# Sliding-window attention: the values of two groups of heads in one go, and the output projection some steps later

## Chip, core and metric

The kernel runs on one core of a Trainium2 chip. The metric is the device time of one launch in microseconds (us), the median of three runs. The change touches one phase of a kernel of two transformer layers.

## What is computed

Two layers; each computes x + s * silu(ffn(xn)) with s an attention and xn the layer norm of x. The change is in the first layer's attention, on B = 2 sequences of S = 2048 tokens, D = 512, 16 heads of 32:

```python
k = (xn @ Wkv @ Wk); v = (xn @ Wkv @ Wv); q = xn @ Wq        # split into 16 heads
mask = (ki <= qi) & ((qi - ki < 128) | (ki < 16))            # a window, and 16 persistent keys
scores = einsum('bqhd,bkhd->bhqk', q, k) * 32 ** -0.5
attn = softmax(where(mask, scores, min))
s = einsum('bhqk,bkhd->bqhd', attn, v).reshape(B, S, D) @ Wo
```

The rest (experts of the first layer, a similarity attention and a shared and routed feed-forward of the second) runs in other phases, before and after.

## The kernel before

`phase_attend` works on 32 tiles of 128 queries. A tile has 16 heads, and each head is one *step*; the program of every engine is one unrolled list over the steps `s`, and `tile_of(s, offset)` gives the tile `u` whose step number `offset` (counted from its first head) is `s`. Work at offsets of 16 and more therefore falls between the heads of the following tile. Each engine executes its list in order, and engines wait for each other by semaphores.

What a head takes, by name:

- `score(s)` (TensorE, line 873): q times the keys of two blocks and the persistent ones, over 96 rows (three parts of 32), 288 columns. It is issued three steps ahead, and there are three PSUM banks for it (`SR = 3`), so it waits until L1033 of the score three before is done.
- `top(s)` (VectorE, L1033): scale, mask and row extremum, in one custom instruction. It needs a buffer that `exps` of three heads before must have read.
- `exps(s)` (ScalarE, L978): the exponential with its row sum; issued two steps ahead of `turn`.
- `turn(s)` (TensorE, L890): at each odd head four 128x128 transposes for two heads.
- `copy_out` (L1044 on VectorE, L988 on ScalarE for pairs 1, 3 and 5): the transposed probabilities to SBUF.

And per tile: `values(u, g)` (L903) multiplies the probabilities of four heads with their values; each of its eight multiplies has 32 columns of weights and writes its own 32 partitions of `psO`, in two passes, so sixteen are issued. `turn_sums` (L913) transposes the persistent keys' probabilities and the inverse row sums, `sums_out` (ScalarE, L994) copies them to `xT`, `spread` (L931) multiplies the inverse sums with a 0/1 matrix `sel` so that each head's inverse stands in its 32 partitions (`psR`, in the bank `psXY`), `inverse_out` (L1000) copies that, `pers_values` (L919) adds the persistent keys' part, `divide` (VectorE, L1057) forms `o`, `out_hi` (ScalarE, L1006) and `out_lo` (VectorE, L1061) split it in two parts, `project(u, c)` (L105 to L107, in the helper `mm3`) multiplies with Wo for c = 0 to 3 into `psXY`, and `finish` (L1068) copies the result. GpSimd gathers the persistent probabilities (L805), scatters token numbers for the later phase (L810) and stores the result (L827).

In steps of the running tile, modulo 16, the order is now: the third `values` of the tile before at 0, `turn_sums` at 1, `spread` at 3, the last `values` and `pers_values` at 4, `divide` at 5, `out_hi` and `out_lo` at 6, the first `values` of this tile at 8, the four parts of `project` at 9 to 12, the second `values` at 12 ahead of the last part, `finish` at 13. Within a step TensorE's order is score, turn, then these.

Waits that matter: `values(u, 0)` waits for `o_ready` of the tile before, since both use `psO`; `spread` waits for `x_out`; `project(u, 0)` waits for `o_split`.

Of the kernel before, what the change touches and what calls it, by code (L numbers as in the profile page):

```python
# [20 lines left out]
P = 128  # L21
# [11 lines left out]
NH, HD = 16, 32  # L33
# [574 lines left out]
def phase_attend(nc, env):  # L608
# [6 lines left out]
    ctx, sb, ps, sem = scope(nc)  # L615
# [4 lines left out]
    GH = 4  # L620
    NGR = NH // GH
# [10 lines left out]
    with ctx:  # L632
# [3 lines left out]
        kp = sb("a_kp", [ST, B, NH, PERSIST], F32R)  # L636
        vd = sb("a_vd", [P, B, 2, HD])
        vp = [sb(f"a_vp{i}", [P, 2, HH, HD]) for i in range(B)]
        sel = sb("a_sel", [NH, NGR, GH, HD])
        mask = [sb(f"a_mask{i}", [P, W]) for i in range(4)]  # L640
        rl = [sb(f"a_rl{i}", [P, P]) for i in range(2)]
        wo = [sb(f"a_wo{h}", [P, KC, D], F32R) for h in range(2)]
# [110 lines left out]
        xT = [sb(f"a_xT{i}", [P, 3 * P]) for i in range(2)]  # L753
# [16 lines left out]
        X_AT = 17  # L770
# [22 lines left out]
        def tile_of(s, offset):  # L793

            u, rest = divmod(s - offset, NH)
            return u if rest == 0 and 0 <= u < TILES else None
# [61 lines left out]
        def _(pe):  # L858
# [66 lines left out]
            def spread(u):  # L925
                pe.wait_ge(x_out, u + 1)
                if u:

                    pe.wait_ge(y_ready, u)
                for g in range(NGR):  # L930
                    ins = pe.matmul(psR[:, g, :], sel[:, g, :, :].rearrange("p j d -> p (j d)"),  # L931
                                    xT[u % 2][0:NH, 2 * P:3 * P], start=True, stop=True)
                ins.then_inc(spread_full, 1)

            def project(u, c):
# [11 lines left out]
            for s in STEPS:  # L947
                if s + SR < N:
                    score(s + SR)
                if s < N:  # L950
                    turn(s)
                for g in range(NGR):
                    if (u := tile_of(s, GH * g + GH - 1 + LAG)) is not None:
                        values(u, g)
                if (u := tile_of(s, X_AT)) is not None:
                    turn_sums(u)
                if (u := tile_of(s, X_AT + 2)) is not None:
                    spread(u)
                if (u := tile_of(s, X_AT + 3)) is not None:
                    pers_values(u)  # L960
                for c in range(KC):
                    if (u := tile_of(s, X_AT + 8 + c)) is not None:
                        project(u, c)

        @block.scalar
        def _(act):
# [23 lines left out]
            def sums_out(u):  # L990
                act.wait_ge(x_full, u + 1)
                if u >= 2:
                    act.wait_ge(pers_done, u - 1)
                act.activation(xT[u % 2][:, :], bank(u, HH)[:, 0:3 * P], ACT.Copy).then_inc(x_out, 1)  # L994
# [15 lines left out]
            for s in STEPS:  # L1010
                if s + SR - 1 < N:
                    exps(s + SR - 1)
                if s < N:
                    copy_out(s)
                if (u := tile_of(s, X_AT)) is not None:
                    sums_out(u)
                if (u := tile_of(s, X_AT + 3)) is not None:
                    inverse_out(u)
                if (u := tile_of(s, X_AT + 5)) is not None:
                    out_hi(u)  # L1020

        @block.vector
        def _(dve):
# [50 lines left out]
            for s in STEPS:  # L1074
                if s + SR < N:
                    top(s + SR)
                if (u := tile_of(s, X_AT - 3)) is not None:
                    invert(u)
                if s < N:
                    copy_out(s)  # L1080
                if (u := tile_of(s, X_AT + 4)) is not None:
                    divide(u)
                if (u := tile_of(s, X_AT + 5)) is not None:
                    out_lo(u)
                if (u := tile_of(s, X_AT + 12)) is not None:
                    finish(u)


# [1581 lines left out]
```

## Time and profile before

| | |
|---|---|
| median of three runs | 4498.79 us (4495.98 to 4507.62) |
| the profiled execution | 4549.09 us, span 4547.1 us |
| TensorE, weight loads | busy 4214.5 us, 3571.8 us |
| VectorE, ScalarE, GpSimd | busy 2097.8, 1663.2, 1354.6 us |
| granted TensorE clock, mean | 0.955 |
| the loop of `phase_attend` | about 398 to 958 us of the span |

Busy times of TensorE include a modelled end of each multiply, so neighbours overlap and the sum is above the time in which it issues. A number in square brackets behind an instruction in a timeline is the idle time of its engine before it, and after the arrow what ended it. Consecutive instructions of one kind are merged, with their count.

### The profile page before, as it was taken

What the parts mean: (1) busy time and instruction counts of PE and PEld (TensorE: products, weight loads), DVE (VectorE), ACT (ScalarE), POOL (GpSimd) and SP (SyncE); (2) the same over time, 40 slices, a digit from 0 to 9 for tenths busy, and PEclk for the clock granted to TensorE, in tenths of its full rate; (3) what the DMA queues carried; (4) which work ended last, traced back from release to release, by engine and by line L of the source; (5) the groups of instructions that cost most, each with busy time, mean ns of one, the idle gap of its engine ahead of it and who ended that gap; (6) DMA issues with size and microseconds to landing.
All of it is one profiled execution on the core that took longest, in us unless ns stands there. A gap on an engine that the chain in (4) does not pass through costs nothing. (4 is left out here: it accounts for less than half of the span.)

```text
span 4547.1 us, 69223 instructions
## 1 busy us (share of the span) xinstructions
PE 4214.5 (93%) x23045; PEld 3571.8 (79%) x23046; DVE 2097.8 (46%) x4010; ACT 1663.2 (37%) x3234; POOL 1354.6 (30%) x2020
## 2 busy tenths in 40 slices
PE   6975888879999999999997999998799999999998
PEld 5864666669989999998985777776578888788887
DVE  4457666644444444444444544453343333343333
ACT  2214666644334444444432333331232222222222
POOL 0012444445555555555551233333100000000000
PEclk8877999989999999999998999998899999999999
DMA  5767676636555556555554533431423222321221
GB/s 188 282 237 173 118 141 122 126 88 131 114 122 124 128 121 135 123 125 128 120 118 140 181 123 130 140 134 58 146 75 104 98 87 71 102 95 63 98 82 48
DMA packets 351911, 561.40 MB, mean 123 GB/s; under 512 B 33089, under 2 KB 198625, under 8 KB 347490
## 3 DMA queue, kind: packets, MB, share of 16 engines
q1 hardware_dynamic: 282770, 394.19, 29.3%
q0 software_dynamic: 68944, 164.62, 16.8%
q8 instruction: 120, 1.97, 0.2%
q14 instruction: 77, 0.63, 0.1%
HBM read 384.36 MB, written 174.34 MB: 123 GB/s over the span
## 5 line engine op out<-in xcount | busy, mean ns | idle before, releaser
L1227 POOL DMA_INDIRECT acc_d<-e_yw,e_to x208 | 336.0, 1615 | 284.9 <-ACT e_yw L1384 268.4
L2289 POOL DMA_DIRECT2D out<-d_res x32 | 17.4, 543 | 1304.8 <-DVE d_res L2521 1304.8
L2468 DVE TENSOR_TENSOR d_h<-d_sg,d_psU 128x512 f32<-128x512 f32 x144 | 98.9, 687 | 520.3 <-PE d_psU L107 461.9
L978 ACT ACTIVATE a_pr<-a_sm,a_nmax 128x272 f32<-128x272 f32 x512 | 264.0, 516 | 167.1 <-DVE a_nmax L1033 137.6
L105 PE MATMUL e_psG<-e_gu,e_xT 128*128 128x352 f32 x832 | 289.6, 348 | 11.4 <-DVE e_xT L1438 9.3
L1446 DVE TENSOR_TENSOR e_h<-e_sg,e_psU 128x352 f32<-128x352 f32 x208 | 108.3, 521 | 394.3 <-ACT e_sg L1397 379.9
L1033 DVE CUSTOM_DVE_ANT_0 a_sm<-a_psS,a_mask 128x272 f32<-128x272 f32 x512 | 212.7, 432 | 156.6 <-PE a_psS L873 140.2
L107 PE MATMUL e_psG<-e_gu,e_xT 128*128 128x352 f32 x832 | 271.9, 327 | 0.0
L106 PE MATMUL e_psG<-e_gu,e_xT 128*128 128x352 f32 x832 | 271.4, 326 | 0.0
L105 PE MATMUL e_psU<-e_gu,e_xT 128*128 128x352 f32 x832 | 271.0, 326 | 0.0
L106 PE MATMUL e_psU<-e_gu,e_xT 128*128 128x352 f32 x832 | 269.6, 324 | 0.0
L105 PE MATMUL e_psY<-e_wd,e_hT 128*128 128x512 f32 (+1 forms) x624 | 265.7, 426 | 1.2 <-DVE e_hT L1429 1.2
L107 PE MATMUL e_psU<-e_gu,e_xT 128*128 128x352 f32 x832 | 266.3, 320 | 0.0
L1197 POOL DMA_INDIRECT e_xs<-xn_d,e_idx x209 | 210.2, 1006 | 174.3 <-POOL e_idx L1194 168.3
L2396 ACT ACTIVATE d_hT<-d_h 128x512 fp32r<-128x512 f32 x144 | 91.0, 632 | 458.9 <-DVE d_h L2468 400.9
L107 PE MATMUL e_psY<-e_wd,e_hT 128*128 128x512 f32 (+1 forms) x624 | 247.1, 396 | 0.0
L1397 ACT ACTIVATE e_sg<-e_psG 128x352 f32<-128x352 f32 x208 | 96.4, 463 | 409.3 <-PE e_psU L107 406.5
L106 PE MATMUL e_psY<-e_wd,e_hT 128*128 128x512 f32 (+1 forms) x624 | 245.4, 393 | 0.0
L2390 ACT ACTIVATE d_sg<-d_psG 128x512 f32<-128x512 f32 x144 | 86.0, 598 | 423.0 <-PE d_psG L107 423.0
L1378 ACT ACTIVATE e_hT<-e_psH 128x384 fp32r<-128x384 f32 x208 | 102.1, 491 | 371.3 <-PE e_psY L107 199.5
L105 PE MATMUL d_psG<-d_x,d_gu 128*128 128x512 f32 x576 | 225.2, 391 | 12.6 <-DMA d_x<-xT_d 12.5
L105 PE MATMUL d_psU<-d_x,d_gu 128*128 128x512 f32 x576 | 227.5, 395 | 0.0
(429 smaller groups left out, 12067.1 us busy)
## 6 DMA issues: line engine op xcount, KB each, us to landing
d_gu_raw<-in_wgu SPq DMA_DIRECT2D x144, 512.0 KB, 3.2
qk_d<-f_qk SPq DMA_DIRECT2D x32, 1024.0 KB
a_q<-qk_d SPq DMA_DIRECT2D x96, 256.0 KB
a_k<-qk_d SPq DMA_DIRECT2D x96, 256.0 KB
e_rawgu<-in_w_gate SPq DMA_DIRECT2D x32, 704.0 KB
e_rawgu<-in_w_up SPq DMA_DIRECT2D x32, 704.0 KB
b_gu_raw<-in_wgu SPq DMA_DIRECT2D x40, 512.0 KB, 3.9
xT_d<-f_xT SPq DMA_DIRECT2D x16, 1024.0 KB
```

Of the source, the lines that this page charges most:

```text
L105: pe.matmul(out, lhs[0], rhs[1], start=first, stop=False, **kw)
L106: pe.matmul(out, lhs[1], rhs[0], start=False, stop=False, **kw)
L107: return pe.matmul(out, lhs[0], rhs[0], start=False, stop=last, **kw)
L978: act.activation(pr[half][:, h % HH, :], sm[s % SR][:, :], ACT.Exp, bias=nmax[s % SR][:, :], scale=-1.0, accum_out=rs[u % 2][:, h:h + 1]). ...
L1033: dve.tensor_tensor_reduce(out=sm[s % SR][:, :], in0=psS[s % SR][:, PERSIST:2 * KW], in1=m[:, :], scale=-SCALE, scalar=3.0e38, op0=ALU.add ...
L1197: pool.indirect_dma_start(rows[:, :], None, env.xn_d, bass.IndirectOffsetOnAxis(ap=idx[k][:, :].bitcast(U32), axis=0))\
L1227: pool.indirect_dma_start(env.acc_d, bass.IndirectOffsetOnAxis(ap=to[:, :].bitcast(U32), axis=0), yw[:, :], None, compute_op=ALU.add).then ...
L1378: act.activation(hT[0][:, :, :], psH[:, :, :], ACT.Copy).then_inc(hT_hi, 1)
L1397: act.activation(sg[:, :], psG[:, 0:M], ACT.Silu).then_inc(sg_ready, 1)
L1446: dve.tensor_tensor(hv[:, :], sg[:, :], psU[:, 0:M], ALU.mult).then_inc(h_ready, 1)
L2396: act.activation(h2[q % 2][0][:, :], hv[q % 2][:, :], ACT.Copy).then_inc(h_hi, 1)
L2468: ins = dve.tensor_tensor(hv[q % 2][:, :], sg[q % 2][:, :], psU[:, :], ALU.mult)
```

## The change

`values` of groups 0 and 1 are issued together at the step of group 1 (12), those of groups 2 and 3 together at the step of group 3 (4 of the next tile). `spread` moves from step 3 to 4, behind that pair; `pers_values` and `inverse_out` from 4 to 5; `divide` from 5 to 6; `out_hi` and `out_lo` from 6 to 7; the four parts of `project` from 9 to 12 to 11 to 14; `finish` from 13 to 15. `sel` has 128 rows instead of 16, the added ones zero, and `spread` multiplies all 128 rows of `xT`.

```diff
--- before.py
+++ after.py
@@ -636,7 +636,7 @@
         kp = sb("a_kp", [ST, B, NH, PERSIST], F32R)
         vd = sb("a_vd", [P, B, 2, HD])
         vp = [sb(f"a_vp{i}", [P, 2, HH, HD]) for i in range(B)]
-        sel = sb("a_sel", [NH, NGR, GH, HD])
+        sel = sb("a_sel", [P, NGR, GH, HD])
         mask = [sb(f"a_mask{i}", [P, W]) for i in range(4)]
         rl = [sb(f"a_rl{i}", [P, P]) for i in range(2)]
         wo = [sb(f"a_wo{h}", [P, KC, D], F32R) for h in range(2)]
@@ -929,7 +929,7 @@
                     pe.wait_ge(y_ready, u)
                 for g in range(NGR):
                     ins = pe.matmul(psR[:, g, :], sel[:, g, :, :].rearrange("p j d -> p (j d)"),
-                                    xT[u % 2][0:NH, 2 * P:3 * P], start=True, stop=True)
+                                    xT[u % 2][:, 2 * P:3 * P], start=True, stop=True)
                 ins.then_inc(spread_full, 1)
 
             def project(u, c):
@@ -949,17 +949,19 @@
                     score(s + SR)
                 if s < N:
                     turn(s)
-                for g in range(NGR):
+
+                for g in range(1, NGR, 2):
                     if (u := tile_of(s, GH * g + GH - 1 + LAG)) is not None:
+                        values(u, g - 1)
                         values(u, g)
                 if (u := tile_of(s, X_AT)) is not None:
                     turn_sums(u)
-                if (u := tile_of(s, X_AT + 2)) is not None:
+                if (u := tile_of(s, X_AT + 3)) is not None:
                     spread(u)
-                if (u := tile_of(s, X_AT + 3)) is not None:
+                if (u := tile_of(s, X_AT + 4)) is not None:
                     pers_values(u)
                 for c in range(KC):
-                    if (u := tile_of(s, X_AT + 8 + c)) is not None:
+                    if (u := tile_of(s, X_AT + 10 + c)) is not None:
                         project(u, c)
 
         @block.scalar
@@ -1014,9 +1016,9 @@
                     copy_out(s)
                 if (u := tile_of(s, X_AT)) is not None:
                     sums_out(u)
-                if (u := tile_of(s, X_AT + 3)) is not None:
+                if (u := tile_of(s, X_AT + 4)) is not None:
                     inverse_out(u)
-                if (u := tile_of(s, X_AT + 5)) is not None:
+                if (u := tile_of(s, X_AT + 6)) is not None:
                     out_hi(u)
 
         @block.vector
@@ -1078,11 +1080,11 @@
                     invert(u)
                 if s < N:
                     copy_out(s)
-                if (u := tile_of(s, X_AT + 4)) is not None:
+                if (u := tile_of(s, X_AT + 5)) is not None:
                     divide(u)
-                if (u := tile_of(s, X_AT + 5)) is not None:
+                if (u := tile_of(s, X_AT + 6)) is not None:
                     out_lo(u)
-                if (u := tile_of(s, X_AT + 12)) is not None:
+                if (u := tile_of(s, X_AT + 14)) is not None:
                     finish(u)
```

## Rows read from the trace of the kernel before

**Rows 1.** Busy time by engine, granted clock, DMA: the loop of `phase_attend`.

```profile
398.00:950.00 552.00, 485.45 (x4532) 382.35 (x4532) 359.56 (x1289) 379.18 (x1196) 237.52 (x384) 0.98 0.61 117
```

**Rows 2.** Tile `a_psXY`: count, duration ns min/median/max, first and last start.

```profile
L931 PE MATMUL a_psXY<-a_xT,a_sel x256: 270/270/372, 408.6 to 948.7; 16*128 16x128 f32 x128
...
L106 PE MATMUL a_psXY<-a_wo,a_oT x128: 391/396/632, 417.2 to 957.3; 128*128 128x512 f32 x128
```

**Rows 3.** Timeline of TensorE, one tile: start us, us, instruction, idle before.

```profile
467.70 0.66 PE L890 MATMUL a_psP<-ident,a_pr 128*128 128x128 f32 x4
468.12 0.48 PE L105 MATMUL a_psXY<-a_wo,a_oT 128*128 128x512 f32 x1
...
471.02 0.30 PE L873 MATMUL a_psS<-a_k,a_q 96*128 96x288 f32 x1
471.25 0.65 PE L903 MATMUL a_psO<-a_pT,a_v 128*32 128x128 f32 x16
471.82 0.50 PE L105 MATMUL a_psXY<-a_wo,a_oT 128*128 128x512 f32 x1
...
472.62 0.30 PE L873 MATMUL a_psS<-a_k,a_q 96*128 96x288 f32 x1
472.75 0.60 PE L890 MATMUL a_psP<-ident,a_pr 128*128 128x128 f32 x4
473.11 0.52 PE L873 MATMUL a_psS<-a_k,a_q 96*128 96x288 f32 x2
...
474.30 0.64 PE L903 MATMUL a_psO<-a_pT,a_v 128*32 128x128 f32 x16
475.16 0.40 PE L873 MATMUL a_psS<-a_k,a_q 96*128 96x288 f32 x1 [0.22 <-DVE a_nmax L1033]
...
476.52 0.27 PE L913 MATMUL a_psP<-ident,a_rl 128*128 128x128 f32 x1
...
478.72 1.15 PE L931 MATMUL a_psXY<-a_xT,a_sel 16*128 16x128 f32 x8 [0.83 <-ACT a_xT L994]
...
480.13 0.64 PE L903 MATMUL a_psO<-a_pT,a_v 128*32 128x128 f32 x16
480.71 1.16 PE L919 MATMUL a_psO<-a_xT,a_vp 128*128 128x128 f32 x8
...
483.98 0.64 PE L903 MATMUL a_psO<-a_pT,a_v 128*32 128x128 f32 x16 [0.70 <-DVE a_o L1057]
...
485.47 0.48 PE L105 MATMUL a_psXY<-a_wo,a_oT 128*128 128x512 f32 x1
```

**Rows 4.** Timeline of VectorE, then of ScalarE, the same tile.

```profile
470.19 0.69 DVE L1044 COPY a_pT<-a_psP 128x512 f32<-128x512 f32 x1 [0.98 <-remote]
...
473.06 0.44 DVE L1033 CUSTOM_DVE_ANT_0 a_sm<-a_psS,a_mask 128x272 f32<-128x272 f32 x1 [1.11 <-PE a_psS L873]
...
477.53 0.44 DVE L1033 CUSTOM_DVE_ANT_0 a_sm<-a_psS,a_mask 128x272 f32<-128x272 f32 x1 [0.99 <-PE a_psS L873]
...
483.15 0.68 DVE L1057 TENSOR_TENSOR a_o<-a_psO,a_rb 128x512 f32<-128x512 f32 x1
...
468.80 0.51 ACT L978 ACTIVATE a_pr<-a_sm,a_nmax 128x272 f32<-128x272 f32 x1
469.21 0.18 ACT L978 ACTIVATION_READ_ACCUMULATOR a_pr<-a_sm,a_nmax 128x1 f32 x1
...
478.18 0.49 ACT L994 ACTIVATE a_xT<-a_psP 128x384 f32<-128x384 f32 x1 [0.99 <-PE a_psP L913]
...
483.87 0.63 ACT L1006 ACTIVATE a_oT<-a_o 128x512 fp32r<-128x512 f32 x1 [0.54 <-DVE a_o L1057]
```

**Rows 5.** Timeline of TensorE and VectorE in tile 0.

```profile
401.53 0.40 PE L873 MATMUL a_psS<-a_k,a_q 96*128 96x288 f32 x1
...
402.88 0.44 DVE L1033 CUSTOM_DVE_ANT_0 a_sm<-a_psS,a_mask 128x272 f32<-128x272 f32 x1 [1.01 <-PE a_psS L873]
```

**Rows 6.** The view of rows 1 for one later stretch.

```profile
538.00:556.00 18.00, 16.30 (x144) 13.03 (x143) 11.38 (x41) 11.64 (x38) 8.27 (x13) 0.91 0.65 126
```

## Prediction

> **What bounds the kernel now.** I read the stretches first: the attention loop takes 552 us of the span, and in it the modelled busy times are TensorE 485 us, ScalarE 379 us, VectorE 360 us [rows 1]. Nothing outside the loop is touched. Its period comes from the first multiply of `spread` in the first and the last tile: (948.7 - 408.6)/31 = 17.42 us for 31 periods [rows 2]. Then the timeline of TensorE over one tile. Written as engine time between starts, one tile's issue is: 16 scores at 0.13 (472.62 to 472.75), 8 `turn`s at 0.36 (to 473.11) and 0.42 where one starts from a wait (467.70 to 468.12), `turn_sums` 0.33 (three transposes at the `turn`'s 0.11), four `values` at 0.57 (471.25 to 471.82), `spread` and `pers_values` 0.9 each (1.15 and 1.16 us less the 0.27 of the last pass), projection four times 0.71 to 0.80 (471.82 to 472.62 is the longest): 12.8 us, some 13.4 with what stands between kinds [rows 2, 3]. So some 4 us of each period TensorE waits, and the loop is a ring of waits: score, L1033, L978, turn, next score but three.
>
> Two waits stand out in rows 3: 0.83 us before `spread` (for `a_xT`) and 0.70 us before `values(u, 0)` at 483.98 (for `a_o`). The first has an odd history. `turn_sums` was issued at 476.52, yet ScalarE starts the copy of it at 478.18, and VectorE the next L1033 at 477.53 though its score was issued at 475.16 [rows 3, 4]. Elsewhere L1033 follows its score by 0.44 us (472.62 to 473.06). The lateness also comes after `values(u, 0)`: a `turn` issued at 467.70 is copied at 470.19 [rows 3, 4]. Completions are late after `values` whose next instruction is a score, and prompt after `values` followed by full 128-row, 128-column multiplies: 471.25 by L105, 480.13 by L919. Position in the tile is not the reason: in tile 0, where no projection runs yet, `values(0, 1)` is followed by a score at 401.53, and that score's L1033 starts at 402.88 [rows 5]. I read this as the column-tiled `values` leaving the array in a state that scores and transposes do not clear promptly; that reading is inference, the lateness is in the rows.
>
> **The change part by part.** *Pairs of `values`.* The same 16 issues per group, in two pairs. From score to `values` takes 0.23 us (471.02 to 471.25) instead of 0.13, and from `values` to the next multiply 0.57, while its sixteen passes start within 0.38 (0.65 less the last pass's 0.27) [rows 2, 3]. So a boundary pair costs 0.10 + 0.20 = 0.30, and two of four go: -0.6 us of TensorE time per tile, worth that only where TensorE is what all wait for. Here one of the two lies in the projection stretch (worth it), the other behind waits. The Trainium skill, TensorEngine Tiling (Array Packing), Tiling Modes, says that changing the tiling mode, not merely the tile, drains the engine. That agrees with the 0.2 us steps; by it alone the sum would be 32 x 0.6 = 19 us, an estimate, and it says nothing of completions that come 1.5 us late.
>
> *`sel` on 128 rows.* The four multiplies stream 128 columns each, as before; the nearest row, L919 with 128 rows, has 1.16 us for its eight passes, L931 with 16 rows 1.15 [rows 3]. Cost between 0 and 0.1 us; I take 0. The added rows of `xT` come from the cleared part of `rl`. The one-time clearing covers the same elements per row: 0. It puts a full-array multiply behind `values(u, 3)`, and `project(u, 1)` stands behind the other pair: the late completions should be gone except in tile 0.
>
> *Steps moved.* `values(u, 0)` is four steps later, `divide` one, so its wait of 0.70 is gone. `spread` has one more step and a pair of `values` before it. But `project` moves two steps, `divide`, `out_hi` and `out_lo` one, so one more pair of scores must pass between `out_lo` and the projection. No DMA is moved within SP's program; the store of `y` on POOL waits two steps more, behind scatters, with POOL busy 237 of 552 us [rows 1]: 0.
>
> I laid the new queues out for one tile, with durations from rows 3 and 4: L1033 0.44 (0.36 where the next starts behind its main part), a copy 0.69 (0.60 likewise), L978 0.51 and, with the reading of its sum, about 0.6 to its release, `out_hi` 0.63; where an instruction's successor may start before it ends, I took the spacing between starts. The estimates to two digits are those of the arithmetic, not of my certainty. Three stretches:
>
> (a) End of projection to `pers_values`. Now 480.71 - 472.62 = 8.09. New: VectorE does L1033 of score 18, a copy, `finish`, and starts score 19's at 2.04; it releases 2.49, L978 3.13, `turn` 3.18; ScalarE then has `sums_out`, so score 20's L978 is done at 4.02; the pair of `values` runs 4.07 to 5.04, `spread` 0.89, score and turn 0.49: **6.42**.
>
> (b) `pers_values` to projection. Now 485.47 - 480.71 = 4.76. New: `divide` starts 1.77 after `pers_values` (behind score 25's L1033), ready 2.47; ScalarE is at L978 and a copy until 2.86, `out_hi` to 3.50; VectorE waits 0.8 us with `out_lo` at its head, does it 3.52 to 4.12, then L1033 of score 27 (4.57), L978 (5.21), the `turn` (5.70): **5.70**. What is queued behind `out_lo` is the L1033 on which score 30 waits: this is the wait that takes the place of the one before `values(u, 0)`.
>
> (c) Projection. Now 472.62 - 468.12 = 4.50, with one `values`. New: 0.78 + 0.13 + 1.07 + 0.80 + 0.13 + 0.36 + 0.78 + 0.13 + 0.71 = **4.89**.
>
> Sum 17.01 against 17.35 for this tile and 17.42 in the mean: -0.42 x 31 = -13 us. First tile and tail: the same chain behind the last score, 0. The profiled execution took 4549.09 us (span 4547.1), 50 above the median of the runs; I carry the difference over: 4536 there, **4486 us** on the median of 4498.79.
>
> **Rivals.** *R1, the waits vanish and none comes.* Then each period loses the wait before `spread` (0.83), that before `values(u, 0)` (0.70) and 0.6 of boundaries: -2.1 x 31 = -66 us, 4433 [rows 3]. Against it: the ring of score, L1033, L978 and turn stays, and (b) has a new wait by the order of the queues. Half of it, 4466, is possible if VectorE catches up during (c).
>
> *R2, the clock.* Slower. In the loop the granted clock is 0.98, with single stretches at 0.91: the 1.2 GHz level instead of 2.4 [rows 1, 6]. The new order has a thinner stretch: in (b), from 1.6 us after the start of `pers_values` to its end, it issues four scores and two `turn`s in 4 us. A fall that follows lands in the projection, where L106 takes 632 instead of 396 ns [rows 2]: 12 such multiplies are 2.8 us at most; I estimate 1.5, about half of the stretch. It decides from the point where more than one tile in four falls (0.42/1.5); with two in three, +0.58 x 31 = 18 us: 4517. For it: rows 6 and the 1.5 us in (b) in which the score behind `out_lo` cannot start. Against: full-row `spread` now stands next to the pair.
>
> *R3, no measurable change*, by a price off by 0.2 us per tile, or because only boundary steps off the ring are saved: 4492 to 4505. *R4, the late completions stay behind the pairs* (they depend on something other than the next multiply): (a) is then about 1 us longer, +0.6 x 31: 4517.
>
> **Numbers.** Forecast (4480 to 4491) 0.40, R1 and its half 0.20, R3 0.18, R2 0.15, R4 0.07. A difference of 0.3%, 13.5 us, is about what a measurement can tell here, and the forecast sits on it: half of it and all of R1 make faster 0.43, the rest of it and R3, less what tails off, same 0.32, R2 and R4 with a tail slower 0.25. Range 4445 to 4519: from beyond the half of R1 to both slower cases; beyond it lie R1 in full and a clock that falls in nearly every tile.
>
> **What would show it.** Right: L913 to L994 and each score to its L1033 within some 0.5 us; no wait for `a_o` at L903; VectorE idle before L1061 of about 0.8 us and TensorE idle before the score two steps later; periods of L931 near 17.0. Wrong: L931 still waiting for `a_xT` behind late sums (R4); granted clock under 0.95 in the loop with L106 above 500 ns in the mean (R2); periods under 16 with no idle before L1061 (R1). The prediction fails if the hand-laid order has VectorE or ScalarE free where the chip has them waiting.

## The result: 1.1% slower, and the profile after

| | before | after |
|---|---|---|
| median | 4503.2 us (4495.98 to 4512.76, 4 runs) | 4556.74 us (4552.21 to 4561.56, 4 runs) |
| profiled execution | 4549.09 us, span 4547.1 us | 4558.72 us, span 4556.9 us |

The ratio is 1.0114, with an interval of 1.0100 to 1.0129: 53.5 us slower, where 4486 us was forecast and the range ended at 4519. The two profiled executions are only 10 us apart, the medians 53. So the profile of before on which the prediction rests came from an execution 46 us above its own median. A second profile of the same kernel (4502.65 us, the first experiment below) is the fair partner; I call it *the second profile of before*.

Lines behind 950 of the new kernel stand two further down: L1035 for L1033, L980 for L978, L1063 for L1061. First the tile `a_psXY`, as in rows 2, of the kernel after:

```profile
L931 PE MATMUL a_psXY<-a_xT,a_sel x256: 275/275/377, 406.7 to 968.9; 128*128 128x128 f32 x128
...
L106 PE MATMUL a_psXY<-a_wo,a_oT x128: 388/399/628, 414.8 to 976.2; 128*128 128x512 f32 x128
```

and of the second profile of before:

```profile
L931 PE MATMUL a_psXY<-a_xT,a_sel x256: 269/270/421, 404.0 to 913.6; 16*128 16x128 f32 x128
```

The mean period is (968.9 - 406.7)/31 = 18.14 us after, (913.6 - 404.0)/31 = 16.44 before, and 17.42 in [rows 2]. 1.70 x 31 = 53 us: the whole loss lies in this loop. (These means run from the first pass of the first `spread` to the last pass of the last one. The periods of single tiles below are spacings between starts in the timelines; the last tile's is shorter.)

One tile of the kernel after, TensorE, for comparison with [rows 3]:

```profile
469.75 0.48 PE L105 MATMUL a_psXY<-a_wo,a_oT 128*128 128x512 f32 x1
...
470.76 1.08 PE L903 MATMUL a_psO<-a_pT,a_v 128*32 128x128 f32 x32
471.77 0.50 PE L105 MATMUL a_psXY<-a_wo,a_oT 128*128 128x512 f32 x1
...
474.68 0.30 PE L873 MATMUL a_psS<-a_k,a_q 96*128 96x288 f32 x1
...
479.77 1.16 PE L931 MATMUL a_psXY<-a_xT,a_sel 128*128 128x128 f32 x8
480.68 0.38 PE L873 MATMUL a_psS<-a_k,a_q 96*128 96x288 f32 x1
...
481.34 1.06 PE L919 MATMUL a_psO<-a_xT,a_vp 128*128 128x128 f32 x8
...
486.01 0.37 PE L873 MATMUL a_psS<-a_k,a_q 96*128 96x288 f32 x1 [1.39 <-DVE a_nmax L1035]
...
486.98 0.48 PE L105 MATMUL a_psXY<-a_wo,a_oT 128*128 128x512 f32 x1
...
487.99 1.93 PE L903 MATMUL a_psO<-a_pT,a_v 128*32 128x128 f32 x32
489.85 0.80 PE L105 MATMUL a_psXY<-a_wo,a_oT 128*128 128x512 f32 x1
490.44 0.63 PE L106 MATMUL a_psXY<-a_wo,a_oT 128*128 128x512 f32 x1
```

and VectorE in the middle of it:

```profile
484.81 0.69 DVE L1063 TENSOR_TENSOR a_oT<-a_o,a_oT 128x512 fp32r<-128x512 f32 x1 [0.73 <-ACT a_oT L1008]
485.42 0.43 DVE L1035 CUSTOM_DVE_ANT_0 a_sm<-a_psS,a_mask 128x272 f32<-128x272 f32 x1
```

Two things are to be seen. The forecast wait is there (0.8 us were forecast for VectorE): VectorE sits 0.73 us with `out_lo` at its head, the reduction of score 27 is queued behind it, and TensorE waits 1.39 us in front of the score that needs that reduction's bank. The wait for `a_o` in front of `values(u, 0)` is gone, as forecast. One sign named for a right forecast did not come: `turn_sums` starts its last transpose at 476.19 and its copy starts at 477.73, 1.54 us later instead of some 0.5. Nothing completes late there; ScalarE starts the copy without idle time, behind an exponential that had waited for VectorE. And at 487.99 the clock has fallen: the pair of `values` takes 1.93 us, where at 470.76 it took 1.08; the multiplies of 512 columns behind it take 0.63 and 0.80 instead of 0.40 and 0.50. Over the whole loop L106 takes 440 ns in the mean; the sign named for R2 asked for over 500. Granted clock (the figure behind the five busy times) and DMA, kernel after:

```profile
480.00:486.00 6.00, 4.39 (x34) 3.81 (x34) 3.69 (x12) 4.13 (x14) 3.59 (x7) 1.00 0.91 182
486.00:492.00 6.00, 5.80 (x50) 4.47 (x51) 2.20 (x10) 3.12 (x11) 2.15 (x3) 0.72 0.80 128
```

A tile without such a stretch has a period of 17.22 to 17.25 us, one with it 18.5 to 18.8; from the fourth tile on they come in the pattern one without, two with.

### The profile page after: what moved, and what is told of

Read it like the earlier page. It is cut to its first block and busy times, and to the rows that moved or that the text cites. A ratio compares the mean times of both kernels' runs of the same rounds, so it can differ in the third digit from the quotient of the medians.

```text
span 4556.9 us, 69287 instructions
## 1 busy us (share of the span) xinstructions
PE 4204.9 (92%) x23045; PEld 3579.1 (79%) x23046; DVE 2100.4 (46%) x4010; ACT 1660.0 (36%) x3234; POOL 1351.6 (30%) x2020
## 5 line engine op out<-in xcount | busy, mean ns | idle before, releaser
L980 ACT ACTIVATE a_pr<-a_sm,a_nmax 128x272 f32<-128x272 f32 x512 | 264.0, 517 | 226.4 <-DVE a_nmax L1035 226.0
L1035 DVE CUSTOM_DVE_ANT_0 a_sm<-a_psS,a_mask 128x272 f32<-128x272 f32 x512 | 212.7, 437 | 184.7 <-PE a_psS L873 179.0
L106 PE MATMUL e_psG<-e_gu,e_xT 128*128 128x352 f32 x832 | 271.4, 326 | 0.0
L106 PE MATMUL e_psU<-e_gu,e_xT 128*128 128x352 f32 x832 | 269.5, 324 | 0.0
L873 PE MATMUL a_psS<-a_k,a_q 96*128 96x288 f32 x512 | 170.6, 355 | 96.6 <-DVE a_nmax L1035 66.7
L106 PE MATMUL e_psY<-e_wd,e_hT 128*128 128x512 f32 (+1 forms) x624 | 245.4, 393 | 0.0
```

Source lines behind the costliest of these rows:

```text
L106: pe.matmul(out, lhs[1], rhs[0], start=False, stop=False, **kw)
L873: pe.matmul(psS[s % SR][:, :].rearrange("p (a k) -> p a k", a=2), qs[u % QR][:, h, :], ks[:, lo:hi + 1:hi - lo, h, :], start=True, stop=Tr ...
L980: act.activation(pr[half][:, h % HH, :], sm[s % SR][:, :], ACT.Exp, bias=nmax[s % SR][:, :], scale=-1.0, accum_out=rs[u % 2][:, h:h + 1]). ...
L1035: dve.tensor_tensor_reduce(out=sm[s % SR][:, :], in0=psS[s % SR][:, PERSIST:2 * KW], in1=m[:, :], scale=-SCALE, scalar=3.0e38, op0=ALU.add ...
```

## The experiments

Each ran beside the kernel before on the same chip. "Period" is the mean from the rows of `spread`, as above. Four chips took part; experiments 1 to 4 and 9 to 12 ran on one, 5 to 8 on a second, 13 to 15 on a third, 16 and 17 on a fourth.

| run | time, us | before beside it | ratio, interval | period |
|---|---|---|---|---|
| e1 before again | 4501.28 | 4499.63 | 0.9999 (0.9989 to 1.0008) | 16.44 |
| e2 after, filled | 4521.91 | 4499.63 | 1.0051 (1.0034 to 1.0068) | 17.15 |
| e3 128 rows only | 4488.82 | 4499.63 | 0.9969 (0.9959 to 0.9980) | 16.05 |
| e4 pairs only | 4602.58 | 4499.63 | 1.0238 (1.0211 to 1.0264) | 19.82 |
| e5 after, no pairs | 4524.89 | 4539.98 | 0.9968 (0.9958 to 0.9978) | 17.04 |
| e6 after, 16 rows | 4574.64 | 4539.98 | 1.0079 (1.0062 to 1.0096) | 18.67 |
| e7 128 rows, one pair | 4507.90 | 4539.98 | 0.9933 (0.9917 to 0.9950) | 16.55 |
| e8 128 rows, projection later | 4523.37 | 4539.98 | 0.9963 (0.9953 to 0.9973) | 17.13 |
| e9 after again | 4557.86 | 4502.41 | 1.0123 (1.0106 to 1.0140) | 18.14 |
| e10 e3 again | 4491.52 | 4502.41 | 0.9977 (0.9967 to 0.9987) | 16.06 |
| e11 values ahead of turn | 4492.14 | 4502.41 | 0.9970 (0.9958 to 0.9981) | 16.06 |
| e12 e7 again | 4513.25 | 4502.41 | 1.0021 (1.0012 to 1.0031) | 16.73 |
| e13 e5 again | 4516.34 | 4503.77 | 1.0027 (1.0016 to 1.0039) | 16.82 |
| e14 pairs, 128 rows, filled | 4518.95 | 4503.77 | 1.0032 (1.0022 to 1.0042) | 17.00 |
| e15 first values later | 4524.61 | 4503.77 | 1.0038 (1.0024 to 1.0053) | 16.97 |
| e16 second values in a wait | 4464.79 | 4503.81 | 0.9908 (0.9891 to 0.9925) | 15.30 |
| e17 e6 again | 4572.66 | 4503.81 | 1.0154 (1.0137 to 1.0171) | 18.68 |

**e1: the kernel before, unchanged.**

> The kernel before, unchanged: what two timings and two profiles of one program differ by. The profiled execution of before took 4549 us, its other runs 4496 to 4513. Ratio 1.000 within 0.3%. If the 46 us of that one execution came from the clock somewhere, this profile shows other stretches at the 1.2 GHz level than the first; in the attention loop it should show few such stretches again (7 of 31 periods of L931 above 17.9 us then).

The time is that of its other runs there, and the trace is not that of [rows 3]. The stretches at the lower clock that were expected did not come again: in the loop up to the last `spread` there is none, where the first profile has eight, and five periods above 17.9 us by the starts (the expectation counts seven). The second profile of before, TensorE:

```profile
460.11 0.48 PE L105 MATMUL a_psXY<-a_wo,a_oT 128*128 128x512 f32 x1
...
464.60 0.30 PE L873 MATMUL a_psS<-a_k,a_q 96*128 96x288 f32 x1
...
465.80 0.38 PE L873 MATMUL a_psS<-a_k,a_q 96*128 96x288 f32 x1
466.28 0.64 PE L903 MATMUL a_psO<-a_pT,a_v 128*32 128x128 f32 x16
467.14 0.40 PE L873 MATMUL a_psS<-a_k,a_q 96*128 96x288 f32 x1 [0.22 <-DVE a_nmax L1033]
467.79 0.66 PE L890 MATMUL a_psP<-ident,a_pr 128*128 128x128 f32 x4 [0.24 <-ACT a_pr L978]
...
468.50 0.27 PE L913 MATMUL a_psP<-ident,a_rl 128*128 128x128 f32 x1
...
469.21 0.66 PE L890 MATMUL a_psP<-ident,a_pr 128*128 128x128 f32 x4 [0.18 <-ACT a_pr L978]
469.80 1.15 PE L931 MATMUL a_psXY<-a_xT,a_sel 16*128 16x128 f32 x8
470.88 0.40 PE L873 MATMUL a_psS<-a_k,a_q 96*128 96x288 f32 x1
...
471.79 1.16 PE L919 MATMUL a_psO<-a_xT,a_vp 128*128 128x128 f32 x8
...
475.06 0.65 PE L903 MATMUL a_psO<-a_pT,a_v 128*32 128x128 f32 x16 [0.70 <-DVE a_o L1057]
...
476.55 0.48 PE L105 MATMUL a_psXY<-a_wo,a_oT 128*128 128x512 f32 x1
```

and its ScalarE:

```profile
469.07 0.47 ACT L994 ACTIVATE a_xT<-a_psP 128x384 f32<-128x384 f32 x1
```

`turn_sums` issued its last transpose at 468.50, its copy started at 469.07, and `spread` waited for nothing: no late completion, and no 0.83 us wait in any tile but the last (0.58 us there). The period is 16.45 to 16.48 in nearly all of them. From the end of the projection to `pers_values` it is 471.79 - 464.60 = 7.19 us, against 8.09 in [rows 3]; from there to the projection 4.76, as in [rows 3].

The late completions can be counted: the reductions that found VectorE waiting for their score and started over 0.9 us after it. In the first profile there are 57 of them in the phase (the longest 2.9 us), in e5, e7 and e8, which ran on the second chip, 57, 19 and 62 (up to 3.1 us); in e6 on that chip, which has pairs, one (0.96 us); in this profile and in those of all other experiments none.

**e2: the kernel after with extra multiplies.** Six 128x128 by 512 multiplies a tile in steps 8 to 10, into the projection's bank before it is written; they change no output.

```diff
+            def fill(u, c):
+                if c == 0:
+                    pe.wait_ge(r_ready, u + 1)
+                    pe.wait_ge(wo_split, 1)
+                pe.matmul(psXY[:, :], wo[0][:, c, 0:P], wo[0][:, c, :], start=True, stop=True)
...
+                for c in range(3):
+                    if (u := tile_of(s, X_AT + 7 + c)) is not None:
+                        fill(u, 0)
+                        fill(u, 1)
```

> The changed kernel with six extra multiplies per tile (128x128 by 512 columns, result thrown away) in the steps 8 to 10, where TensorE waits for the score behind out_lo. Theory C (the clock: the changed order lets TensorE's clock fall to 1.2 GHz in two tiles of three, and the slow multiplies then lie in the projection): the granted clock stays at 1.00 in the loop, the periods of 18.6 to 18.8 us go to about 17.2, and the kernel is faster than the changed one by about 30 us, near the one before. Theory W (the new wait behind out_lo itself costs the time): the periods stay, and the kernel is as slow as the changed one or slower by up to 6 x 0.21 x 31 = 39 us.

More work, 35 us less time. The granted clock of the loop, in the view of [rows 1], in this kernel

```profile
398.00:950.00 552.00, 497.58 (x4725) 401.42 (x4716) 360.89 (x1279) 373.00 (x1187) 235.02 (x383) 1.00 0.60 118
```

and in the kernel after

```profile
398.00:950.00 552.00, 467.88 (x4345) 381.86 (x4344) 348.94 (x1245) 363.31 (x1158) 226.95 (x370) 0.94 0.59 116
```

Every tile now has a period of 17.22 to 17.25, that of the undisturbed tiles of the kernel after. So the clock at its lower level, 1.2 instead of 2.4 GHz, is worth (18.14 - 17.15) x 31 = 31 us in the loop, of 35 between the medians, and 22 us over before remain, for the new order itself.

**e3: only the 128 rows of `sel` and `xT`** (the first two hunks of the change).

> Only the 0/1 matrix of spread on 128 rows, all else as before. Theory L (late completions come when values are followed by a score): nothing changes, since no values stand before spread; L913 to L994 still 1.6 us, time within 0.3% of before. Rival: the 16-row multiplies are what makes completions late or the clock fall, then the wait before L931 shrinks below 0.3 us and the kernel is 20 to 40 us faster.

10.8 us faster, and e10 gave 10.9 again (4491.52 against 4502.41). Neither expectation came: it is more than the 0.3% of the first by a hair, and half of what the rival asks, without a wait that it could shorten. TensorE in e3:

```profile
468.09 0.66 PE L890 MATMUL a_psP<-ident,a_pr 128*128 128x128 f32 x4 [0.18 <-ACT a_pr L978]
468.58 1.06 PE L931 MATMUL a_psXY<-a_xT,a_sel 128*128 128x128 f32 x8
469.39 0.38 PE L873 MATMUL a_psS<-a_k,a_q 96*128 96x288 f32 x1
```

`turn` to `spread` is 0.49 us, 0.59 in the second profile of before; `spread` to the next score 0.81, 1.08 there. Together 0.37 of the 0.39 us by which the tile got shorter. The Trainium skill, TensorEngine Tiling (Array Packing), Tiling Modes, says that a change of tiling mode drains the engine, and lists tiles of 32 rows by 128 columns among the modes. That a multiply on 16 rows runs in such a mode is my reading; the gaps on both sides of it agree with that, and no run here shows the mode itself. I had named that rule for the 32-column `values` and had not applied it to the 16-row `spread`.

**e4: only the pairs.** In all steps of before; spread on 16 rows.

```diff
-                for g in range(NGR):
+                for g in range(1, NGR, 2):
                     if (u := tile_of(s, GH * g + GH - 1 + LAG)) is not None:
+                        values(u, g - 1)
                         values(u, g)
```

> Only the pairs of values (groups 0 and 1 at step 12, 2 and 3 at step 4), spread, pers_values, divide and projection where they were, 16 rows in the matrix of spread. Theory L: both pairs are followed by full-array multiplies, so the completions are prompt, L913 to L994 within 0.5 us, the wait before L931 gone, the period 16.3 to 16.6 us instead of 17.42: 25 to 35 us faster than before. Theory W (the completions have nothing to do with what follows values): still late, at most 0.6 us per tile gained, 0 to 19 us faster. Theory C would make it slower if the shorter waits still leave the clock falling in more tiles than before: 0.5 to 1 us per period more, periods of 17.5 and more beside short ones.

103 us slower, the worst of all: the theory of late completions had forecast 25 to 35 us faster, and the one of the clock 0.5 to 1 us a period. Before the clock fell (the first three periods) the period was 17.34 to 17.42, and 17.35 is 0.89 over the kernel before; later it was about 20.4 in most tiles. TensorE in e4 in such a tile:

```profile
511.08 0.37 PE L873 MATMUL a_psS<-a_k,a_q 96*128 96x288 f32 x1 [1.06 <-DVE a_nmax L1034]
...
513.93 2.07 PE L931 MATMUL a_psXY<-a_xT,a_sel 16*128 16x128 f32 x8
515.93 0.61 PE L873 MATMUL a_psS<-a_k,a_q 96*128 96x288 f32 x1
516.47 1.94 PE L903 MATMUL a_psO<-a_pT,a_v 128*32 128x128 f32 x32
518.34 2.00 PE L919 MATMUL a_psO<-a_xT,a_vp 128*128 128x128 f32 x8
...
522.81 0.37 PE L873 MATMUL a_psS<-a_k,a_q 96*128 96x288 f32 x1 [1.06 <-DVE a_nmax L1034]
```

The two idle stretches of 1.06 us stand where before the third group's and the first group's `values` had been. `spread`, the pair and `pers_values` then run at the lower clock: 2.07, 1.94 and 2.00 us, where at the full one they take 1.15, 1.08 and 1.16.

**e5 and e13: after without the pairs** (moves and 128 rows stay). The second run because of the chip, see e9.

```diff
-                for g in range(1, NGR, 2):
+                for g in range(NGR):
                     if (u := tile_of(s, GH * g + GH - 1 + LAG)) is not None:
-                        values(u, g - 1)
                         values(u, g)
```

> The kernel after with each group's values in a step of its own again (the third of four in the step where it stood before); the inversions, the copies and the projection keep their new steps and the spread of the inverses its 128 rows. Theory: the pairs leave TensorE without filling work in front of two scores and carry nearly all of the cost; the moved steps are worth what is left over, 17.24 - 16.46 of the kernel after, less 0.89 of the pairs alone, plus 0.39 of the 128 rows, so 0.28 us a tile: period 16.07 + 0.28 = 16.35, no stretch of low clock in the loop, about 4498 us. Rival: the moved steps make the wait in front of the score that meets the difference on VectorE's queue, and it is the main loss: period near 17.2 and 4520 or more, or 4550 if the clock falls too.

> The kernel after with each group's values in a step of its own again, once more. Theory: the moved steps alone open no wait, since the values of the third group fill TensorE's idle time in front of the score that meets the difference on VectorE's queue: period 16.07 to 16.35 on the chip where the kernel before takes 4500 us, so 4489 to 4498. Rival: they cost what the run beside the slower kernel before showed, a period of 17.05 and 4520 us on either chip.

In e13 20 tiles have 16.34 to 16.36, as forecast (16.35), but ten have 17.8 to 17.9 with a stretch at the lower clock. So the moves cost 0.28 us a tile undisturbed (16.35 against the 16.07 of e3), and with them alone some tiles already fall to the lower clock; by it the time, 4516.34, lies above the forecast 4489 to 4498. On e5's chip no clock fell in the loop, but the period was 17.05: the copy of `turn_sums` starts 1.38 us behind it in the median, 0.77 in e13. The forecast 4498 was missed there too, and the rival's 4520 came, with another cause than the rival's wait.

**e6 and e17: after with `spread` on 16 rows.**

```diff
-        sel = sb("a_sel", [P, NGR, GH, HD])
+        sel = sb("a_sel", [NH, NGR, GH, HD])
...
-                                    xT[u % 2][:, 2 * P:3 * P], start=True, stop=True)
+                                    xT[u % 2][0:NH, 2 * P:3 * P], start=True, stop=True)
```

> The kernel after with the spread of the inverses on 16 rows again. Theory: the mode switch costs here what it cost in the order of before, 0.39 us a tile, so an undisturbed period of 17.24 + 0.39 = 17.63 and 12 us more than after, 4569 us, if as many tiles fall to the low clock. Rival: in the new order the spread stands in a step with slack, in front of a wait that ends at the same time whatever the spread takes, and the period stays at 17.24 and the time at 4557.

> The kernel after with the spread on 16 rows, once more. Theory: behind a pair of values the multiply on 16 rows costs only what stands behind it, 1.08 us to the next score against 0.91, so an undisturbed period of 17.41 and 0.17 x 31 = 5 us more than after, plus what the clock does: 4563 to 4575. Rival: the full 0.39 us a tile, 4570 or more with a period of 17.63.

15 to 17 us slower than the kernel after (4557.86 in e9). The undisturbed period is 17.41, between e6's two figures (17.63 and 17.24; e17's expectation was made from it), and only 0.17 above 17.24: from the pair to `spread` it is 1.01 us, as on 128 rows, and from `spread` to the next score 1.08 against 0.91. But with it nearly every tile is one with a lower clock (granted 0.91 in the loop), and that makes most of the time.

**e7 and e12: 128 rows and one pair** (the third and fourth group; the first two stay).

```diff
-                    if (u := tile_of(s, GH * g + GH - 1 + LAG)) is not None:
+                    if g != 2 and (u := tile_of(s, GH * g + GH - 1 + LAG)) is not None:
+                        if g == 3:
+                            values(u, 2)
                         values(u, g)
```

> The kernel before with the spread on 128 rows and only the values of the last two groups of heads as a pair; the first two stay apart and nothing else is moved. Theory: taking the third group's values out of its step opens the wait of TensorE there, 1.05 us against 0.22 in the kernel with both pairs: 0.83 us a tile less the 0.30 of two mode switches saved, period 16.07 + 0.53 = 16.60, 16 us over the kernel with 128 rows alone, about 4505 us; with the clock at its lower level in some tiles more. Rival: the cost of the pairs comes from the first pair, or from the delay of the divide behind both pairs, and this one is near 16.1 and 4489 us.

> The kernel before with the spread on 128 rows and the last two groups' values as a pair, once more. Theory: it has no values in front of a score at the place where the late completion delays the spread, so its time does not go with the chip: 4505 to 4510 us on each, which is 8 us slower than the kernel before where that takes 4500 and 32 us faster where it takes 4540.

The undisturbed period is 16.50: +0.43 over e3 (0.53 was forecast), half of what both pairs cost. On e12's chip five stretches fell to the lower clock, on e7's one before the last tile, and e12 took 4513.25 where 4505 to 4510 were forecast.

**e8: 128 rows and the projection one step later.**

```diff
-                    if (u := tile_of(s, X_AT + 8 + c)) is not None:
+                    if (u := tile_of(s, X_AT + 9 + c)) is not None:
                         project(u, c)
...
-                if (u := tile_of(s, X_AT + 12)) is not None:
+                if (u := tile_of(s, X_AT + 13)) is not None:
                     finish(u)
```

> The kernel before with the spread on 128 rows and the projection with its copy out one step later, nothing else. Theory: no step of this part is on the path that sets the period as long as it ends before the turn of the row sums, so the period stays at 16.07 and the time at 4489 us. Rival: the last part of the projection then falls into a step that is full, or the copy out meets another score's reduction on VectorE, and it is 0.2 to 0.5 us a tile longer, 4495 to 4504 us.

Not comparable with e3, since it ran where values complete late; most tiles had 16.5 or 17.4 to 17.5 us, some 16.8 to 17.0. It shows that lateness. TensorE and ScalarE in e8:

```profile
817.54 0.27 PE L913 MATMUL a_psP<-ident,a_rl 128*128 128x128 f32 x1
...
819.78 0.49 ACT L994 ACTIVATE a_xT<-a_psP 128x384 f32<-128x384 f32 x1 [1.08 <-remote]
...
820.33 1.16 PE L931 MATMUL a_psXY<-a_xT,a_sel 128*128 128x128 f32 x8 [0.92 <-ACT a_xT L994]
```

2.24 us from the transposes to their copy (0.57 in the second profile of before), and 0.92 of wait: the picture of [rows 3, 4].

**e9: the kernel after, unchanged.**

> The kernel after once more, unchanged, beside the kernel before on the same chip. Theory: which time the kernel before takes depends on whether the values complete late, and that goes with the chip; the kernel after has no values in front of a score, so no late completions anywhere, and takes 4553 to 4565 us on every chip. So the ratio is 1.011 where the kernel before takes 4500 us, and 1.004 where it takes 4540. Rival: the longer time of the kernel before on one chip is something common to all kernels there, and the kernel after shifts with it: a ratio of 1.011 on each.

It ran on e1's chip, so the other chip was not seen with it; e6 and e17, the kernel after but for the 16 rows, took 4574.64 beside a before of 4539.98 and 4572.66 beside one of 4503.81. So the new order, seen there with 16 rows, does not go with the chip, and the old one does.

**e10: e3 again**, told there. **e11: `values` ahead of `turn` in the step**, with 128 rows:

```diff
-                if s < N:
-                    turn(s)
                 for g in range(NGR):
                     if (u := tile_of(s, GH * g + GH - 1 + LAG)) is not None:
                         values(u, g)
+                if s < N:
+                    turn(s)
```

> The kernel before with the spread on 128 rows once more. Theory: 0.39 us a tile below the kernel before on each chip, 4489 us where that takes 4500; where the values complete late, the group ahead of the projection's last part decides and the gain can be smaller, 4528 to 4540 us where the kernel before takes 4540.

> The kernel before with the spread on 128 rows, and in each step the values ahead of TensorE's wait for the exponentials, not behind it; nothing else moves. Theory: TensorE then has the values as filling work in the idle time ahead of that wait, so where they stand does not add to the path: period 15.8 to 16.07, 4480 to 4489 us. Rival: the values themselves then wait for the copies of the transposes (the later group of two), the score of the next step is not earlier, and the period is 16.07 or, with a new wait, up to 16.6: 4489 to 4505 us.

No difference from e10: an order within the step that moves the filling work inside the same wait gives nothing.

**e14: pairs, 128 rows and the extra multiplies** (`fill` of e2 in the steps `X_AT + 5 + c`).

> The kernel before with the values in pairs, the spread on 128 rows, and six extra multiplies of 512 columns a tile in the steps after the product with the persistent values (into the bank of the projection, before it is written; the extra work changes no output). Theory: they hold the granted clock, so the pairs show their own waits alone: 17.35 - 0.39 = 16.96 us a tile without a low stretch in the loop, 15 us over the kernel before, 4515 us. If so the moved steps add the other 0.27 to reach the 17.24 of the kernel after. Rival: the clock falls all the same, since the idle time in front of the scores is elsewhere: period near 18 or more and 4550 us; or the multiplies are in the way and the period is above 17.24.

The period is 16.94 to 16.97 in 25 of 31 tiles, as forecast (16.96); one tile in the loop fell to the lower clock. Its TensorE at the step of the third group (L874 is the score, L891 `turn`, L904 `values`, L920 `pers_values` here):

```profile
468.86 0.38 PE L874 MATMUL a_psS<-a_k,a_q 96*128 96x288 f32 x1
470.29 0.37 PE L874 MATMUL a_psS<-a_k,a_q 96*128 96x288 f32 x1 [1.06 <-DVE a_nmax L1045]
470.85 0.66 PE L891 MATMUL a_psP<-ident,a_pr 128*128 128x128 f32 x4 [0.19 <-ACT a_pr L990]
...
473.89 1.08 PE L904 MATMUL a_psO<-a_pT,a_v 128*32 128x128 f32 x32
474.90 1.16 PE L920 MATMUL a_psO<-a_xT,a_vp 128*128 128x128 f32 x8
```

In the second profile of before the same stretch, from the score at 465.80 by way of `values` to the transposes at 467.79, took 1.99 us; here, without `values`, it takes 470.85 - 468.86 = 1.99. The group had been free in this step. Pairing it also saved less than the forecast 0.30: in the pair it costs 474.90 - 473.89 = 1.01 instead of 0.57 (471.25 to 471.82 in [rows 3]): +0.44, twice, is the 0.88 (16.95 - 16.07).

**e15: only the first group's values one step later**, 128 rows, no pairs.

```diff
-                    if (u := tile_of(s, GH * g + GH - 1 + LAG)) is not None:
+                    if (u := tile_of(s, GH * g + GH - 1 + LAG + (g == 0))) is not None:
```

> The kernel before with the spread on 128 rows and only the first group's values one step later, no pairs. Theory: the wait for the quotient in front of these values goes, but TensorE then waits as long in front of the next score, whose time the chain of exponentials and reductions sets: period 16.07, 4489 us. Rival: this wait is on the path, and the period is up to 0.5 us shorter, 4474 us; or the values then stand behind the transposes and delay the next score by their 0.6 us.

The wait of 0.70 for `a_o` went, as the prediction counted on, and 0.76 us a tile were lost (16.83 undisturbed). In e15:

```profile
475.57 0.37 PE L873 MATMUL a_psS<-a_k,a_q 96*128 96x288 f32 x1 [1.06 <-DVE a_nmax L1033]
476.29 0.66 PE L890 MATMUL a_psP<-ident,a_pr 128*128 128x128 f32 x4 [0.35 <-ACT a_pr L978]
476.88 0.65 PE L903 MATMUL a_psO<-a_pT,a_v 128*32 128x128 f32 x16
477.45 0.50 PE L105 MATMUL a_psXY<-a_wo,a_oT 128*128 128x512 f32 x1
```

The wait did not vanish; it has another name and stands empty. From the score ahead of it (474.13) to these transposes it is 2.16 us, as in e3 with `values` in between (472.47 to 474.63), and from the transposes to the projection 1.16 instead of the 0.41 of e3: `values` is paid for on top. I had expected 4489 us; the rival with 0.6 us was the nearer one. Three tiles also fell to the lower clock.

**e16: the second group's values into a wait.** The reverse of the change: with 128 rows, they leave the projection and join the third group's step.

```diff
-                    if (u := tile_of(s, GH * g + GH - 1 + LAG)) is not None:
+                    if (u := tile_of(s, GH * g + GH - 1 + LAG + 4 * (g == 1))) is not None:
```

> The kernel before with the spread on 128 rows and the second group's values four steps later, in the step of the third group's and ahead of them, nothing else moved. Theory: they leave the projection, where TensorE waits for nothing and they take 0.57 + 0.23 - 0.13 = 0.67 us, and join the step in front of the score with an idle time of 0.22 and the transposes with one of 0.24, where they add 0.44: 0.46 of it is hidden. So the period is 16.07 - 0.67 = 15.40 to 15.45, 20 us less than with the 128 rows alone, about 4469 us. Rival: the ring of score, reduction, exponential and transposes sets the time of that stretch as well as of the projection's, and nothing or little is gained, 16.07 and 4489; or the clock falls, now that the busy stretch is thinner, and it is 4500 or more.

4464.79 us, 0.9% under before; the forecast was 4469. The period is 15.31, 0.76 under e3, where 15.40 to 15.45 was forecast. TensorE in e16:

```profile
460.51 0.38 PE L873 MATMUL a_psS<-a_k,a_q 96*128 96x288 f32 x1
460.99 1.08 PE L903 MATMUL a_psO<-a_pT,a_v 128*32 128x128 f32 x32
462.00 0.40 PE L873 MATMUL a_psS<-a_k,a_q 96*128 96x288 f32 x1
462.50 0.66 PE L890 MATMUL a_psP<-ident,a_pr 128*128 128x128 f32 x4
```

The pair of `values` takes 1.01 us, yet from the score ahead of it to the transposes it is 1.99 us as with one group and with none; both waits there, 0.22 and 0.24, are gone. This is the fastest version of the study: a pair as in the change, but in the step that waits.

## Why the prediction was wrong

The prediction's own three stretches, as laid out and as measured (before: its second profile; after: the undisturbed tile shown above):

| stretch | now, predicted from | now, e1 | new, predicted | new, measured |
|---|---|---|---|---|
| (a) projection to `pers_values` | 8.09 | 7.19 | 6.42 | 481.34 - 474.68 = 6.66 |
| (b) `pers_values` to projection | 4.76 | 4.76 | 5.70 | 486.98 - 481.34 = 5.64 |
| (c) projection | 4.50 | 464.60 - 460.11 = 4.49 | 4.89 | 474.68 - 469.75 = 4.93 |
| sum | 17.35 | 16.44 | 17.01 | 17.23 |

- **The failing step is the baseline of (a), 8.09 us.** "Completions are late after `values` whose next instruction is a score" was read as a property of the kernel. It is one of some executions: it stands in the first profile (4549.09 us) and in e5, e7 and e8, beside a before of 4540, and not in e1 at 4502.65. The new order is rid of it, as I said (one in e6), but the timed runs of before, 4495.98 to 4512.76, took the time of e1 and, by its trace, had nothing of the kind to lose. That moves the difference of orders from -0.34 to +0.79 us a tile: 24 us slower instead of 11 faster, and e2's 22 us measure it. (The forecast's 13 us took a new tile without a clock stretch from the mean of 17.42, which held eight.)
- **What each error is worth.** A period change of -0.42 was forecast and +1.70 came: 2.12 x 31 = 66 us, of the 71 between 4486 and 4556.74. The baseline is 17.42 - 16.44 = 0.98 of it (30 us), the clock 18.14 - 17.15 = 0.99 (31 us, after against e2), and the hand-laid order 0.15 (4 us): 0.22 in the tile of the table, nearly all of it in (a), less what the shorter last tile takes off the mean. The other 5 us are not accounted for.
- **The clue was in front of me.** 50 us between the profiled execution and the median were "carried over" as if they lay outside the change. They lay mostly in it: (17.42 - 16.44) x 31 = 30 us of 46 between the two spans. About 25 of the 30 are late completions, since the 22 periods without a lower clock still have 17.30 in the mean against 16.46; some 5 are the eight stretches at the lower clock. The others are 4.6 us ahead of the loop (408.6 against 404.0) and 11.3 behind it (4547.1 - 948.7 against 4500.7 - 913.6).
- **The rival of the clock happened.** R2 was given 0.15. Its place, its rate (two tiles in three) and its price (1.5 us) were right: 18.7 - 17.24. Its cause, the score behind `out_lo`, fits e2, where work in that wait kept the clock. It is 31 us of the loop by e2 against after. Looking back, that the stretch lost the first group's `values` as filling was a reason to give it more. With only R2 right and the base wrong, 4517 was 40 us too low.
- **The price of the 128 rows was 0 and is -0.39 us a tile** (e3), a gain of 11 us: it softened the loss by luck, since nothing in the prediction had it. The comparison of 1.15 with 1.16 us for the eight passes was of the wrong thing; the cost stands in the gaps before and behind.
- **That pairs save 0.30 at each boundary was nearly so, and beside the point.** A group alone takes 0.67 us (0.57 and the 0.10 in front), in the pair 0.44: 0.23 saved. The pairs cost 0.88 us a tile all the same: e14 minus e3, again the first periods of e4 minus e1 (0.89), and again e2 minus e13 (17.24 - 16.35 = 0.89). The two groups that were moved had stood in waits, where they cost nothing; in the pair each costs 0.44.
- **The moves**: the new wait of (b) is as forecast, but the gain from moving `values(u, 0)` was none (e15). All moves together cost 0.28 (e13 undisturbed against e3).

The parts add up: 16.46 - 0.39 (rows) + 0.88 (pairs) + 0.28 (moves) = 17.23 us, measured 17.22 to 17.25. Taken one after the other (e3, e13, after) the steps must add up; the check is that the pairs cost the same without the moves, in e14 and e4. With the clock's share it is 18.14, so 1.70 x 31 = 53 us.

What stays open: why `values` completes late on one chip and not on three others, with the same program. That it goes with the chip is what 18 runs of before there (4533.56 to 4552.9) and 68 on the others (4495.37 to 4514.13) suggest; but that chip was seen in one session only, and something else of that session isn't excluded. What makes completions late was not found, and the reading that `values` leaves the array in a state that scores do not clear was not tested. Which chip the first profile came from isn't known; its picture is that of e8. That the clock falls because of the thin stretch ahead is shown as far as e2 goes: work put there keeps it. Why some tiles fall and others with the same waits don't (one in three in the kernel after, 20 of 30 in e13) is open.

## What to carry to other kernels

When the profiled execution's time is far from the median, find where the difference lies before costing anything; a second profile of the unchanged kernel settles it. Work that stood inside a wait was free here, and taking it out to merge it with other work makes it cost time while the wait stays: before moving an instruction, ask what ends the wait around it, not only what it waits for itself. Merge toward the wait, as e16 does, not toward the busy stretch.

## What was not expected of the hardware

- The same kernel took 4540 us on one chip and 4500 to 4504 on three. Traces from that chip show late completions behind 32-column `values` followed by a score (in e8 2.24 us from transposes to their copy instead of 0.57). The order with `values` before other multiplies took nearly the same there and elsewhere (4574.64 and 4572.66).
- Six more multiplies a tile made the kernel 35 us faster, by the granted clock: 1.00 against 0.94 over the loop. The longest wait in front of the falls was 1.39 us.
- Behind transposes, the four multiplies on 16 rows cost 0.10 us more ahead and 0.27 us more behind than the same on 128 rows, while their last pass took 0.27 us either way; behind a pair of 32-column `values` it was nothing ahead and 0.17 us behind (e6, e17).
